# A perceiver block on one core: cross attention's scores from high and low halves of one pair's keys and queries, value weights loaded pair by pair

## The reference, cut to what matters

```python
k, v = split(ctx @ w_kv_x.T)                # per batch entry: 1601 rows, 8 groups of 128 each
k = layernorm(k) * kxln_w + kxln_b
scores = q @ k.T / sqrt(128)                # 2 heads x 64 queries = 128 rows by 1601 columns
p = softmax(scores)
out = p @ v                                 # written here as (p @ ctx) @ w_v of the group
```

## Time and profile before

| what | value |
|---|---|
| median of three runs | 2853.08 us |
| the profiled execution | 2851.99 us |
| its span | 2850.2 us |
| TensorE matmul busy | 2671.0 us (94%) |
| TensorE weight loads busy | 2168.2 us (76%) |
| VectorE busy | 1787.3 us (63%) |
| ScalarE busy | 1504.6 us (53%) |
| GpSimd busy | 473.4 us (17%) |
| DMA | 303.10 MB, mean 106 GB/s |

### The profile page before, as it was taken

How to read it: one execution, slowest core, us unless ns; L and a number is a source line. 1 busy time by engine, 2 the same in 40 slices (tenths; PEclk the granted TensorE clock), 3 DMA queues, 4 the chain that set the end, 5 groups by cost and what they waited for, 6 DMA issues and landing times.

```text
span 2850.2 us, 38665 instructions
## 1 busy us (share of the span) xinstructions
PE 2671.0 (94%) x13446; PEld 2168.2 (76%) x13446; DVE 1787.3 (63%) x4741; ACT 1504.6 (53%) x2919; POOL 473.4 (17%) x392
## 2 busy tenths in 40 slices
PE   6889999999999999999999999989998878959999
PEld 4678787787787787787787877768777778747887
DVE  6847438447357356365284375668668685558997
ACT  6945326336235244254263363446675567837776
POOL 3402002002011011021020020024332222011111
PEclk9989999999999999999999999999999999979999
DMA  3442012012021030030020121525666632529996
GB/s 122 133 146 84 3 36 85 4 55 66 4 69 51 5 93 23 13 89 9 24 83 4 46 64 41 197 75 168 168 180 180 149 63 76 186 84 392 377 374 232
DMA packets 238816, 303.10 MB, mean 106 GB/s; under 512 B 127640, under 2 KB 156952, under 8 KB 225312
## 3 DMA queue, kind: packets, MB, share of 16 engines
q1 hardware_dynamic: 235824, 296.36, 32.2%
q0 software_dynamic: 2800, 4.27, 0.6%
HBM read 259.48 MB, written 46.98 MB: 108 GB/s over the span
## 4 chain that ended last, share of the span: by engine, by line
PE 76%; DVE 11%; ACT 6%; issue 3%; DMA 2%; SPq 2%; POOL 1%; POOLq 0%; DVEq 0%; ACTq 0%
PE ps L103 19%; PE ps L105 18%; PE ps L104 18%; PE ps L773 6%; PE ps L792 3%; PE ps L755 2%; PE ps L822 2%; DVE zz L2032 1%; DVE lnw L2029 1%; DVE cv L1996 1%; PE ps L813 1%; DMA ca<-cat_d 1%; PE ps L512 1%; PE ps L1869 1%; SPq L1692 1%
## 5 line engine op out<-in xcount | busy, mean ns | idle before, releaser
L1151 POOL TENSOR_TENSOR lnw<-lnw,half 128x8 f32<-128x8 f32 x88 | 144.4, 1640 | 1233.0 <-DVE lnw L884 1233.0
L103 PE MATMUL ps<-whf,cth 128*128 128x512 f32 (+1 forms) x832 | 336.2, 404 | 1.6 <-ACT kn L1027 1.6
L103 PE MATMUL ps<-cnh,pth 128*128 128x512 f32 (+1 forms) x832 | 330.3, 397 | 6.5 <-issue 5.5
L105 PE MATMUL ps<-whf,ctl 128*128 128x512 f32 (+1 forms) x832 | 326.1, 392 | 0.0
L104 PE MATMUL ps<-wlf,cth 128*128 128x512 f32 (+1 forms) x832 | 325.1, 391 | 0.0
L105 PE MATMUL ps<-cnh,ptl 128*128 128x512 f32 (+1 forms) x832 | 324.6, 390 | 0.0
L104 PE MATMUL ps<-cnl,pth 128*128 128x512 f32 (+1 forms) x832 | 324.4, 390 | 0.0
L2470 DVE TENSOR_TENSOR ml<-mr,mh 128x2048 fp32r<-128x2048 f32 x90 | 203.4, 2287 | 32.1 <-ACT mh L2414 32.1
L1017 DVE TENSOR_SCALAR pc<-ps,sm 128x512 f32<-128x512 f32 x64 | 48.1, 751 | 277.1 <-PE ps L105 277.1
L1089 ACT ACTIVATE xo<-ps 128x128 f32<-128x128 f32 x64 | 17.7, 277 | 371.1 <-PE ps L822 371.1
L1064 ACT ACTIVATE pr<-ps,sm 128x1601 f32<-128x1601 f32 x56 | 89.6, 1601 | 224.3 <-DVE sm L929 224.3
(11 more groups left out here) (332 smaller groups left out, 6113.5 us busy)
## 6 DMA issues: line engine op xcount, KB each, us to landing
mr<-in_moe SPq DMA_DIRECT2D x90, 1024.0 KB, 6.9
ctr<-in_ctxt SPq DMA_DIRECT2D x96, 256.0 KB, 2.9
pr<-in_ctxn SPq DMA_DIRECT2D x96, 256.0 KB
wr<-in_wqkv SPq DMA_DIRECT2D x64, 256.0 KB, 2.9
wvf<-in_wattn SPq DMA_DIRECT2D x12, 1024.0 KB, 4.9
ca<-cat_d SPq DMA_DIRECT2D x16, 512.0 KB, 4.2
qk_d<-cv SPq DMA_DIRECT2D x32, 256.0 KB, 3.3
wr<-in_wz SPq DMA_DIRECT2D x32, 256.0 KB, 3.3
```

Of the source, the lines that this page charges most:

```text
L103: pe.matmul(dst, lh, rh, start=first, stop=False)
L105: return pe.matmul(dst, ll, rh, start=False, stop=last)
L1151: po.tensor_tensor(rs[0:w, s, :], nv[0:w, s, :], half[0:w, 0:8], ALU.pow).then_inc(kx_rs, 1)
```

## The change

Four edits.

1. Keys and queries of a group now lie side by side in one tile `kq` [128, 8, 1730]: 1601 keys, one spare column, 128 queries. `k_out_ac` writes the last tile 66 columns wide instead of 65.
2. For the pairs g = 2 to 7 of each batch entry (48 of 64) ScalarE copies the 1730 columns of the pair to `kqh` (f32r) and VectorE writes the rest to `kql`. Both halves have room for one pair, so the copy waits until the scores of the pair before are done. It stands in round g-2, behind parts 2 and 3 of the probabilities.
3. `score_pe` for these pairs goes by `three`: twelve f32r matmuls of 512, 512, 512 and 66 columns, three of each, behind one more wait. Pairs 0 and 1 stay as they are.
4. The value weights are no longer loaded at once; `wv` has room for one group, and each pair's 256 KB are loaded when the former pair's result has been copied out. `xo_pe` waits for its own load each time. `wv`, `kqh` and `kql` lie where `wvf` lay.

```diff
+        kq = sb2("kq", [128, 8, SC + 129])
+        kf, qb = kq[:, :, 0:SC + 1], kq[:, :, SC + 1:SC + 129]
...
+        wv = sbv("wv", [128, 4, 128])
+        kqh = sbv("kqh", [128, SC + 129], f32r)
+        kql = sbv("kql", [128, SC + 129], f32r)
...
+        def wv_load(sp, m):
+            sp.dma_start(wv[:, :, :], wv_in[m % 8]).then_inc(d_wv, 16)
...
+        def pair_split_of(m):
+            return 6 * (m // 8) + m % 8 - 1
...
@@ s3_sp
                     if i == 2 and b > 0:
                         xo_store(sp, b - 1, 7)
+                        wv_load(sp, 8 * b)
...
                     if g > 0:
                         xo_store(sp, b, g - 1)
+                        wv_load(sp, 8 * b + g)
...
@@ score_pe
                     pe.wait_ge(p_exp, p_exp_of(m) - 1)
+                if g >= 2:
+                    pe.wait_ge(*kq_low.at(pair_split_of(m)))
...
-            f = pe.matmul(ps[:, o:o + width], qb[:, g, :], kf[:, g, o:o + width], start=True, stop=True)
+            if g >= 2:
+                width += width % 2
+                f = three(pe, ps[:, o:o + width], kqh[:, SC + 1:SC + 129], kql[:, SC + 1:SC + 129],
+                          kqh[:, o:o + width], kql[:, o:o + width], True, True)
+            else:
+                f = pe.matmul(ps[:, o:o + width], qb[:, g, :], kf[:, g, o:o + width], start=True, stop=True)
...
@@ xo_pe
-            if m == 0:
-                pe.wait_ge(d_wv, 32)
+            pe.wait_ge(d_wv, 16 * (m + 2))
             for c in range(4):
-                f = pe.matmul(bank(7)[:, 0:128], wv[:, c, 128 * g:128 * g + 128], pcT[:, c, :], start=c == 0, stop=c == 3)
+                f = pe.matmul(bank(7)[:, 0:128], wv[:, c, :], pcT[:, c, :], start=c == 0, stop=c == 3)
...
+        def kq_high_ac(ac, m):
+            ac.wait_ge(scored, 2 * m)
+            ac.activation(kqh[:, :], kq[:, m % 8, :], ACT.Copy).then_inc(kq_high.sem, 1)
+
+        def kq_low_dv(dv, m):
+            dv.wait_ge(*kq_high.at(pair_split_of(m)))
+            dv.tensor_tensor(kql[:, :], kq[:, m % 8, :], kqh[:, :].bitcast(fp32), ALU.subtract).then_inc(kq_low.sem, 1)
...
@@ s3_dv
                     p_low_dv(dv, b, g, (2, 3))
+                    if g + 2 < 8:
+                        kq_low_dv(dv, m + 2)
...
@@ k_out_ac
             o, w = TILES[i]
+            w += w % 2
...
@@ s3_ac
                     p_high_ac(ac, b, g, (2, 3))
+                    if g + 2 < 8:
+                        kq_high_ac(ac, m + 2)
```

More of the change, by code:

```diff
@@ L117, in program @@
         wlf = sb12("wlf", [128, 4096], f32r)
-        wv, wkh, wkl = (z.rearrange("p (c n) -> p c n", c=4) for z in (wvf[:, :], whf[:, :], wlf[:, :]))
+        wkr, wkh, wkl = (z.rearrange("p (c n) -> p c n", c=4) for z in (wvf[:, :], whf[:, :], wlf[:, :]))
         s1 = ExitStack()
@@ L421, in program @@
         ptl = sb2("ptl", [128, 13, 128], f32r)
-        kf = sb2("kf", [128, 8, SC])
-        qb = sb2("qb", [128, 8, 128])
+        kq = sb2("kq", [128, 8, SC + 129])
+        kf, qb = kq[:, :, 0:SC + 1], kq[:, :, SC + 1:SC + 129]
         pr = sb2("pr", [128, 2, SC])
@@ L434, in program @@
         s12.close()
+        sv = ExitStack()
+        sbv = stack_sb(sv)
+        wv = sbv("wv", [128, 4, 128])
+        kqh = sbv("kqh", [128, SC + 129], f32r)
+        kql = sbv("kql", [128, SC + 129], f32r)
+        sv.close()
         d_wv, d_qb = sem("d_wv"), sem("d_qb")
@@ L455, in s1b_sp @@
             sp.wait_ge(proj, 48)
-            sp.dma_start(wv[:, :, :], wk_in).then_inc(d_wv, 16)
+            sp.dma_start(wkr[:, :, :], wk_in).then_inc(d_wv, 16)
             for n in range(3):
@@ L465, in s1b_sp @@
                     sp.wait_ge(wk_low, 4)
-                    sp.dma_start(wv[:, :, :], wv_in).then_inc(d_wv, 16)
+                    wv_load(sp, 0)
                 if k == 5:
@@ L569, in s1b_dv @@
                     dv.wait_ge(wk_high, k)
-                    dv.tensor_tensor(wkl[:, k - 1, :], wv[:, k - 1, :], wkh[:, k - 1, :].bitcast(fp32),
+                    dv.tensor_tensor(wkl[:, k - 1, :], wkr[:, k - 1, :], wkh[:, k - 1, :].bitcast(fp32),
                                      ALU.subtract).then_inc(wk_low, 1)
@@ L602, in s1b_ac @@
                         ac.wait_ge(d_wv, 16)
-                    ac.activation(wkh[:, k, :], wv[:, k, :], ACT.Copy).then_inc(wk_high, 1)
+                    ac.activation(wkh[:, k, :], wkr[:, k, :], ACT.Copy).then_inc(wk_high, 1)
                 elif k < 6:
@@ L609, in program @@
         kx_half = sem("kx_half")
+        kq_high, kq_low = Again(wk_high, 4), Again(self_co, 8)
         kx_done, kx_var, kx_rs, kx_nm = sem("kx_done"), sem("kx_var"), sem("kx_rs"), sem("kx_nm")
@@ L816, in xo_pe @@
         def xo_pe(pe, m):
-            g = m % 8
             pe.wait_ge(pcT_out, m + 1)
-            if m == 0:
-                pe.wait_ge(d_wv, 32)
+            pe.wait_ge(d_wv, 16 * (m + 2))
             for c in range(4):
-                f = pe.matmul(bank(7)[:, 0:128], wv[:, c, 128 * g:128 * g + 128], pcT[:, c, :], start=c == 0, stop=c == 3)
+                f = pe.matmul(bank(7)[:, 0:128], wv[:, c, :], pcT[:, c, :], start=c == 0, stop=c == 3)
             f.then_inc(xo_done, 1)
@@ L1418, in program @@
         d_gb = [Again(d_ct[0], 560), Again(d_ct[1], 560), Again(d_ct[2], 544), Again(d_cn[0], 832)]
-        d_am, d_z, d_xt = Again(d_wv, 32), Again(d_ca[0], 128), [Again(d_co[0], 64), Again(d_co[1], 64), Again(sem("d_xt2"), 0)]
+        d_am, d_z, d_xt = Again(d_wv, 1040), Again(d_ca[0], 128), [Again(d_co[0], 64), Again(d_co[1], 64), Again(sem("d_xt2"), 0)]
         d_mt = [Again(d_pw[2].sem, 32), Again(d_xo[0], 512)]
@@ L2688, in layout @@
         "x": a["x"].reshape(512, 512), "vec": vec, "row": row, "const": const, "wattn": wattn,
-        "wk": kvt[0], "wv": kvt[1], "ctxt": ctxt, "ctxr": ctxr, "ctxn": ctx,
+        "wk": kvt[0], "wv": kvt[1].reshape(128, 4, 8, 128).transpose(2, 0, 1, 3), "ctxt": ctxt, "ctxr": ctxr, "ctxn": ctx,
         "wproj": X["wproj"].T.reshape(32, 128, 512),
```

## The result

The changed kernel takes 2839.6 us, the median of four runs (2838.71 to 2842.95), beside 2855.57 for the kernel before on the same chip (four runs, 2848.36 to 2861.65). The ratio is 0.9947, 95% interval 0.9921 to 0.9973: some 15 us, or 0.53%, faster. The forecast was 2836 in a range of 2828 to 2850. Each ratio here is to the kernel before as it ran beside the kernel in question; it can differ from the quotient of the two medians by up to 0.001.

The account below looks back on a forecast made before the run. TensorE's issue was taken to bound the kernel in cross attention. From the profiled 2851.99 us, -18 for scores, +0.5 for the last batch entry and +0.3 for loads gave 2834.8; with 1.1 to the median, 2836 us, range 2828 to 2850.

Parts of the forecast that it names:

- The wide matmuls: In a pair's scores, nine f32r matmuls of 512 columns take 2.15 - 0.08 = 2.07 us.
- the 0.08 that the turns in front give back: Four turns ahead of an f32r group take 0.35 us by the next matmul instead of 0.44.
- The narrow ones: In a pair's scores, three f32r matmuls of 66 columns, 0.11 us each, add 0.31 us, bounds 0.21 and 0.72.
- Rival 1: In the scores, each narrow matmul takes a wide slot: 2.75 goes to 2.79 us, total 2856, no change; chance 0.10.
- Weight loads: On TensorE, loads rise from 8 to 12 a pair, issued beside matmuls; nothing added to the time.
- Rival 4: On TensorE, weight loads don't overlap: four more cost 0.44 us a pair against 0.37 gained, total 2857; chance 0.03.
- The splits: ScalarE copy 1.65 us, VectorE subtraction 1.95, with 3.4 us of room before scores; no cost in the first seven entries.
- rival 3: Splits beyond 7.06 us make scores wait, beyond 7.4 slower than before; at 2.3 times the price 2895 us; chance 0.05.
- The last batch entry: Quantization also stands on VectorE, so turns of parts 2 and 3 wait: +0.5 us, bounds 0 and 1 a round.
- Behind the last pair: The last 256 KB of value weights push the projection's loads: 0.3 us where TensorE waits, bounds 0 and 0.7.
- every charge at its upper bound: Total with all charges at their upper bounds and narrow matmuls at 0.11 us: 2846 us.
- rival 2: Bounds of the waits and the last batch entry come true and eat half the gain: 2845 us; chance 0.11.

Follow-up runs that it names:

- experiment 2: Kernel before with only the value weights loaded one pair at a time, scores and keys unchanged: 2855.73 us, ratio 1.0006.
- experiment 8: Experiment 7's kernel with the last pair's result copied out ahead of the next scaling of concatenated heads on ScalarE: 2827.74 us, ratio 0.9912.
- experiment 9: Kernel before with only the last pair's result copied out ahead of the next scaling of concatenated heads: 2850.61 us, ratio 0.9994.
- experiment 10: Changed kernel with only the last pair's result copied out ahead of the next scaling of concatenated heads: 2837.18 us, ratio 0.9947.
- experiment 4: Changed kernel with the last 65 keys of each pair scored in plain fp32 again: 2834.81 us, ratio 0.9937.
- experiment 7: Changed kernel with the last 65 keys in plain fp32 and the last pair's value weights loaded one round earlier: 2833.31 us, ratio 0.9934.
- experiment 3: Changed kernel with its splits, waits and loads kept but all scores in plain fp32, so the splits are not used: 2856.79 us, ratio 1.0012.
- experiment 6: Changed kernel with the last pair's value weights loaded one round earlier, into a tile of their own: 2839.04 us, ratio 0.9952.
- experiment 1: Changed kernel run again with no edit: 2841.11 us, ratio 0.9956.
- experiment 5: Changed kernel with each split's copy and subtraction made twice, one after the other: 2880.39 us, ratio 1.0099.

## Why the prediction was right, and where it was off

**The wide matmuls: right.** 2.07 us forecast; 2.17 less the 0.08 that the turns in front give back, 2.09, measured.

**The narrow ones: right in kind, a little dear.** 0.31 forecast out of 0.21 to 0.72; they take 0.25. The first, whose load lies under the wide matmul before it, is followed after 0.03 us, and the others stand 0.11 apart, as the two loads in the earlier trace rows had it. Rival 1, a wide slot each, is refuted by the round above.

**What the sum left out.** The turns behind an f32r group are slower: five of L818 take 0.60 us, and 0.56 behind plain fp32. The prediction used the same rows to count the turns' gain in front of a group, and not what they lose behind one. 2.09 + 0.25 + 0.04 = 2.38: the errors (0.02 and 0.04 too little, 0.06 too much) cancel, which is luck, and the round fell by 0.35 where 0.37 was forecast. In the first seven batch entries that is 15.0 us against 15.5.

**Weight loads: right.** 78% of the span instead of 76%, with the wide starts still 0.23 apart. Rival 4, and the Trainium skill's rule in "TensorE: Matmul & The Clock Gate", "What overlaps and what doesn't", would have made the round longer than before; it is 0.35 us shorter. Here each load takes all 128 rows and columns and overlaps the matmul in flight (loads of 0.19 us beside starts 0.23 apart), so the measurement stands against the rule.

**The splits: right to 0.01 us in length** (1.650 and 1.962 against 1.65 and 1.95) and right in their cover: 3.5 us of room against 3.4. What the text missed is that the pair at the head of each batch entry has only 2.0 us. The doubled split (7.2 us) confirms the mechanism of rival 3. For pairs 3 to 7 it is just beyond where the prediction had the border, at 7.06 us, and loses 0.31 us a round; for the pair at the head the border is 1.5 us nearer. How the loss grows beyond that was not run.

**The last batch entry: forecast +0.5, measured less.** Here VectorE takes the quantization straight behind the split and then `pc` and `ptl` without a wait, as forecast, but the turns are hardly late:

```profile
1708.66 0.92 PE L818 MATMUL ps<-cst,pr 128*128 128x128 f32 x5
1709.42 0.60 PE L839 MATMUL ps<-cst,pc 128*128 128x128 f32 x4
```

They take 0.76 us instead of 0.60 in this one round, and the later rounds take 14.04. So the term is +0.16. The other 1.2 us that this batch entry kept are the clock in the round of pair 1, for which the sum had no term, and how the change could bring it about stays open.

**Behind the last pair: the step that failed.** The term was "an estimated 0.3 us where TensorE waits for them (bounds 0 and 0.7)". The loads alone cost 0.66 (experiment 2), at the edge of it, but the changed kernel lost 2.1 to 2.6. The step priced a transfer by its bytes and looked only at who waits for the *loads behind it*. It did not look at what a late load holds back in ScalarE's queue: a result that four further steps hang on. Experiments 8 to 10 show this chain. What stays open is the size of its two parts. Some 0.4 us of the first has a place: the load of heads that the first `yb` waits for is issued 10.58 us ahead of the last `xo_pe` where it was 11.01, since the load of value weights stands ahead of it in SyncE's queue. The rest is the time to landing, 11.7 us before and 12.2 after, but 13.6 in experiment 4 and 13.0 in experiment 7, which has no load of 256 KB in that place. Seen from `xo_pe` that `yb` started after 1.6 us in both profiles of the changed kernel, 1.45 with the new loads alone, 2.4 and 2.7 in experiments 3 and 4, and, without the 256 KB in that place, 1.0 in experiment 6 and 2.0 in experiment 7. And the load of heads behind x took 6.4 to 6.7 us in some kernels (before, experiments 2, 3, 4, 7, 9, 10) and 7.7 to 7.9 in others (after, experiments 1 and 6), and no edit goes with it.

**The sum.** 2851.99 - 15.0 (first seven entries) - 0.8 (last) + 2.6 (projection) = 2838.8 in place of 2834.8, and with the 1.1 us to the median 2839.9, where 2839.6 was measured. That this comes within 0.3 us is luck too: the profiled execution of the changed kernel took 2842.95, and the kernel before came out at 2855.57 over four runs instead of 2853.08 over three. As a difference, 17 us were forecast (2853.08 to 2836) and 16 measured (2855.57 to 2839.6). Of the 4.0 us between 2838.8 and 2834.8, 2.3 are the projection and 1.2 the clock in one round; the round at 0.356 for 0.37 adds 0.7 over 48 pairs, and the last entry's +0.16 for +0.5 takes 0.3 back. Two ends of the prediction don't follow from its own bounds: every charge at its upper bound gives 2836 + 5.5 + 0.4 + 5.6 = 2847.5 and not 2846, and rival 2 gives 2847 and not 2845. The forecast doesn't hang on either.

## What to carry to other kernels

Where TensorE sets the time, price a change of a matmul's form by the distances between starts, of the group itself and of what stands ahead of it and behind it; the terms of a gain of 0.35 us in a round could be forecast to 0.02 to 0.06 us each that way. Choose the form for each width: here three f32r matmuls win at 512 columns (0.70 us against 0.86, as long as the splits on the other engines are covered) and two plain fp32 ones at 65 (0.16 against 0.25). And for a transfer added at the end of a stage, follow each engine's queue behind the instruction that waits for it: a small copy whose result starts a chain of loads belongs ahead of one that waits for a DMA, and a cover measured in the middle of a loop is not the cover of its first round.

## What the runs showed of the hardware that was not expected

- The first narrow f32r matmul is followed after 0.03 us, less than any distance of matmuls in the rows ahead of the prediction, and the next two after 0.11. Two fp32 instructions of 65 columns take 0.16 us together.
- Five turns of 128 columns take 0.60 us behind f32r matmuls and 0.56 behind plain fp32. Eight turns take 0.79 ahead of f32r and 0.87 ahead of plain fp32.
- The same eight plain fp32 matmuls took from 3.4 to 4.8 us up to the next start, where the granted clock fell to the lower level behind a stretch in which TensorE was half idle. One such place varies by more than several terms of the sum.
- A wait of 1.5 us was once enough for the lower level: in experiment 5 the wide f32r matmuls behind it started 0.43 us apart for 3 us, and not 0.23. The same wait in the six other batch entries cost no clock.
